# Eight stages and two mixtures of experts: routing rows split by token, the first expert's weights split in the stage in front, routing batches spread

## What is computed

```python
# layer 2: top 2 of 8
probs = softmax(x @ router_w.T); weights, indices = top_k(probs, 2)
weights = weights / (weights.sum() + 1e-6)
h = silu(x @ w13[e][:, :256]) * (x @ w13[e][:, 256:]);  y_e = h @ w2[e]
# layer 3: nucleus, cumulative probability below 0.8, the first always
probs = softmax(x @ Wr + br);  gate = probs * keep
h = relu(x @ W1[e] + b1[e]);   y_e = h @ W2[e] + b2[e]
# both
out = sum over e of gate[:, e] * y_e
```

## Time and profile before

| | us |
|---|---|
| median of 3 runs | 2840.24 (2839.24 to 2847.72) |
| the profiled execution | 2835.16, span 2833.3 |
| stage 6, first to last matmul of the experts | 1428.74 to about 1761 |
| stage 8, the same | 2383.60 to about 2813 |

### The profile page before, as it was taken

One profiled execution on the slowest core, in us unless ns is written; L12 is line 12 of the kernel. 1 busy time (PEld: TensorE's weight loads), 2 busy tenths in 40 slices (PEclk: granted clock), 3 DMA queues, 4 the chain that ended last, 5 costly groups with the idle time before them and its releaser, 6 DMA issues. The chain is left out here.

```text
span 2833.3 us, 35006 instructions
## 1 busy us (share of the span) xinstructions
PE 2458.7 (87%) x12090; PEld 1772.0 (63%) x12090; DVE 1925.9 (68%) x3555; ACT 1459.8 (52%) x3077; POOL 976.1 (34%) x763
## 2 busy tenths in 40 slices
PE   5677778698999999999989998688888886999998
PEld 2554656586888888888867776233333323677776
DVE  6737556776666666666576665499888997766765
ACT  4221222497444444444345555455555553788777
POOL 1000000010222222222025555488888884222221
PEclk8668789899999999999979999799999987999999
DMA  4000000000000000000100000222222230000001
GB/s 172 0 1 0 1 1 1 1 1 15 1 1 1 1 1 1 1 1 1 60 1 1 1 8 0 60 72 84 78 80 82 80 83 15 1 1 1 1 1 30
DMA packets 31169, 66.85 MB, mean 24 GB/s; under 512 B 3200, under 2 KB 7312, under 8 KB 30480
## 3 DMA queue, kind: packets, MB, share of 16 engines
q1 hardware_dynamic: 30960, 64.59, 7.3%
q0 software_dynamic: 32, 0.02, 0.0%
HBM read 61.98 MB, written 2.62 MB: 23 GB/s over the span
## 5 line engine op out<-in xcount | busy, mean ns | idle before, releaser
L192 PE MATMUL ps<-TMPr 128*128 128x512 f32 (+6 forms) x3936 | 1043.1, 413 | 87.0 <-DVE TMPr L208 57.4
L192 PEld LDWEIGHTS ps<-TMPr 128*128 128x128 f32 (+4 forms) x3936 | 736.1, 194 | 402.9 <-issue 176.0
L212 POOL TENSOR_TENSOR TMP<-TMP 128x512 f32<-128x512 f32 (+2 forms) x480 | 619.0, 1314 | 704.3 <-ACT TMP L203 466.3
L192 PE MATMUL ps<-TMP 128*128 128x65 f32 (+4 forms) x4320 | 527.3, 290 | 1.2 <-DVE TMP L207 0.5
L192 PEld LDWEIGHTS ps<-TMP 128*128 128x128 f32 (+3 forms) x4320 | 480.3, 192 | 60.8 <-issue 19.0
L192 PE MATMUL ps<-TMP,W 128*128 128x512 f32 (+5 forms) x720 | 380.6, 655 | 138.6 <-POOL TMP L212 43.3
L203 ACT ACTIVATE TMP<-ps,W 128x256 f32<-128x256 f32 (+2 forms) x512 | 274.4, 580 | 354.7 <-DVE TMP L208 192.7
L208 DVE TENSOR_TENSOR TMP<-ps,TMP 128x512 f32<-128x512 f32 (+1 forms) x434 | 251.4, 603 | 128.0 <-ACT TMP L203 67.8
L192 PEld LDWEIGHTS ps<-TMP,W 128*128 128x128 f32 (+3 forms) x720 | 130.6, 199 | 312.2 <-issue 158.5
L203 ACT ACTIVATE TMPr<-ps,W 128x512 fp32r<-128x512 f32 x352 | 242.4, 689 | 114.4 <-PE ps L192 94.1
L212 POOL TENSOR_TENSOR XT<-XT,XK 128x512 f32<-128x512 f32 x128 | 175.1, 1368 | 324.0 <-DVE XK L211 308.0
(11 more groups left out here) (180 smaller groups left out, 2778.9 us busy)
## 6 DMA issues: line engine op xcount, KB each, us to landing
TMP<-rows SPq DMA_DIRECT2D x168, 256.0 KB, 3.6
W<-wp SPq DMA_DIRECT2D x1, 4124.0 KB, 13.4
W<-wp SPq DMA_DIRECT2D x1, 3072.0 KB, 25.2
W<-wp SPq DMA_DIRECT2D x1, 2136.5 KB, 18.6
XT<-xT SPq DMA_DIRECT2D x4, 512.0 KB, 6.1
out<-XK SPq DMA_DIRECT2D x8, 256.0 KB, 2.3
W<-wp SPq DMA_DIRECT2D x1, 1993.0 KB, 14.2
W<-wp SPq DMA_DIRECT2D x1, 903.0 KB, 9.8
```

The source lines that it names most:

```text
L192: return nc.tensor.matmul(out, lhsT, rhs, start=start, stop=stop, **k)
L212: gtt = lambda o, a, b, op: nc.gpsimd.tensor_tensor(o, a, b, op)
```

## The change

1. **Rows split by token.** Each batch's gate weights are split while tokens are on partitions: DVE casts 128x64 to `WKR` (columns 0 to 7 of each tile's 40) and subtracts for columns 32 to 39. PE turns 40 columns at once, ACT copies all 40 rows to `WT`, and the DVE step of `row` is gone. `gate` waits for the ACT copy (`mw_act`). POOL clears two 128x320 buffers in place of the 40x4096 one.
2. **First expert's weights.** Their high parts are cast on ACT and their low parts subtracted on POOL in the stage in front: at the start of layer norm 5 for stage 6, behind the first norm of stage 7 for stage 8.
3. **Batches and front spread.** The second half of `front` (sum, reciprocal, probabilities) becomes a step at u = 1. Batch 0 stands at u = (2, 2, 2) or (2, 3, 4); batches 1 to 3 at chunks 2, 4, 6. Expert 1's weights come after chunk 5.

```diff
+        def pool(e):
+            if k == 5:
+                first_weights_low(e, 6)
...
-        part = {6: (0, 1, 1), 8: (0, 1, 2)}[k]
+        part, start = {6: (0, 1, 1), 8: (0, 1, 2)}[k], {6: (2, 2, 2), 8: (2, 3, 4)}[k]
...
-                        b = 0 if i == 0 else (i + 1) // 2 if i % 2 else None
-                        if b is not None and b < 4:
-                            plan += [("route", (k, b, r)) for r in range(3) if part[r] == c]
-                        j = i * nd + c - (nd + 1)
+                        u = i * nd + c
+                        if u == 1:
+                            plan.append(("probs", k))
+                        plan += [("route", (k, 0, r)) for r in range(3) if start[r] == u]
+                        if i and i % 2 == 0:
+                            plan += [("route", (k, i // 2, r)) for r in range(3) if part[r] == c]
+                        j = u - (nd + 1)
...
-                if i == 1 and e + 1 < 8:
+                if i == (1 if e else 5) and e + 1 < 8:
                     plan.append(("weights", (k, e + 1)))
...
+    def first_weights_high(e, k):
+        n, u, d = first_w[k]
+        kh = first_wb[k][0]
+        e.wait_ge(s_w[MOE[k]["g"]], 16)
+        acopy(kh[:, 0:512], u)
+        acopy(kh[:, 512:], d).then_inc(*mf_high(k))
+
+    def first_weights_low(e, k):
+        n, u, d = first_w[k]
+        kh, kl = first_wb[k]
+        e.wait_ge(*mf_high.at(k))
+        gtt(kl[:, 0:512], u, kh[:, 0:512].bitcast(F32), ALU.subtract)
+        gtt(kl[:, 512:], d, kh[:, 512:].bitcast(F32), ALU.subtract).then_inc(*mf_low(k))
...
+                high, low = g3(WKR[b % 2], 8)[:, :, 0:8], g3(WKR[b % 2], 8)[:, :, 32:40]
+                e.wait_ge(*at_("scaled" if k == 6 else "kept"))
+                e.wait_ge(*mr_zero.at(k))
+                if b >= 2:
+                    e.wait_ge(*mw_pe.at((k, 2 * b - 3)))
+                copy(high, wk).then_inc(*sig("high"))
+                e.wait_ge(*at_("high"))
+                tt(low, wk, g3(WKF[b % 2], 8)[:, :, 0:8], ALU.subtract).then_inc(*sig("low"))
...
-                        c = 4 * i + j
-                        r = turn(tile(PS[0][0:8, :], j), WK[:, c * 8:c * 8 + 8], w("ident"))
+                        c = 4 * (i % 2) + j
+                        r = turn(tile(PS[0][0:40, :], j), WKF[i // 2 % 2][:, c * 40:c * 40 + 40], w("ident"))
...
-                    e.wait_ge(*mw_dve.at((k, i)))
+                    e.wait_ge(*mw_act.at((k, i)))
...
-                    acopy(ch(WT, a[1])[0:8, :], PS[0][0:8, :]).then_inc(*mw_act(a))
+                    acopy(ch(WT, a[1])[0:40, :], PS[0][0:40, :]).then_inc(*mw_act(a))
...
-            weights(e, 0)
...
-                elif step == "row":
-                    x = ch(WT, a[1])
-                    e.wait_ge(*mw_act.at(a))
-                    minus(x[32:40, :], PS[0][0:8, :], x[0:8, :]).then_inc(*mw_dve(a))
+                elif step == "probs":
+                    probs(e)
...
-            if k == 6:
-                e.wait_ge(*me_w.at((k, 0, "low")))
-                nc.gpsimd.memset(WT.bitcast(F32), 0.0).then_inc(*mr_zero(k))
+            for x in WKF:
+                last = nc.gpsimd.memset(x, 0.0)
+            last.then_inc(*mr_zero(k))
```

More of the change, by code:

```diff
@@ L1738, in build @@
     FRONT = "logits max shifted sum reciprocal probs".split()
-    BATCH = {6: ("top pair pair_reciprocal first", "replaced", "taken kept scaled"),
-             8: ("top cum below always kept_probs", "fill kept_or_fill replaced", "taken kept")}
+    BATCH = {6: ("top pair pair_reciprocal first", "replaced", "taken kept scaled high low"),
+             8: ("top cum below always kept_probs", "fill kept_or_fill replaced", "taken kept high low")}
     LG = mem["TMP"][:, TN - 256:TN]
+    first_w = {6: (768, w("w13")[:, 0:512], w("w2e")[:, 0:256]), 8: (1024, w("W1")[:, 0:512], w("W2")[:, 0:512])}
+    first_wb = {k: [mem["TMPr"][:, TN - 256 - j * n:TN - 256 - (j - 1) * n] for j in (2, 1)] for k, (n, u, d) in first_w.items()}
     def moe_plan(k):
@@ L1792, in build @@
         if st == "front":
-            mr_keys += [(a, "fill")] + [(a, n) for n in FRONT]
+            mr_keys += [(a, n) for n in ["fill"] + FRONT[:3]]
+        elif st == "probs":
+            mr_keys += [(a, n) for n in FRONT[3:]]
         elif st == "route":
@@ L1798, in build @@
     mr_zero = Sig(sem("moe_rows_zeroed"), moe_on)
-    me_w = Sig(sem("moe_weights"), [(k, e, s) for k in moe_on for e in range(8) for s in ("high", "low")])
+    me_w = Sig(sem("moe_weights"), [(k, e, s) for k in moe_on for e in range(1, 8) for s in ("high", "low")])
+    mf_high, mf_low = (Sig(sem("moe_first_weights_" + n), moe_on) for n in ("high", "low"))
     me_sel = Sig(sem("moe_select"), moe_on)
@@ L1817, in build @@
     rows = of(moe_all, "row")
-    mw_pe, mw_act, mw_dve = (Sig(sem("moe_row_" + n), rows) for n in ("pe", "high", "low"))
+    mw_pe, mw_act = (Sig(sem("moe_row_" + n), rows) for n in ("pe", "act"))
     m8_xh, m8_xl = Sig(sem("moe_x_high"), range(NCH)), Sig(sem("moe_x_low"), range(NCH))
     sem.keep()
+    def first_weights_high(e, k):
[10 more added lines that the diff above has]
+        gtt(kl[:, 512:], d, kh[:, 512:].bitcast(F32), ALU.subtract).then_inc(*mf_low(k))
     def moe_stage(k):
@@ L1825, in moe_stage @@
         nw = nu + nd
-        ar, ax = Arena(mem["TMP"], mem["TMPr"], TN - 256), arena_xk()
-        WT, WK = ar(T, 40, FR), ar(256)
-        assert ar.o == XP
+        ar, ax = Arena(mem["TMP"], mem["TMPr"], TN - 256 - 2 * first_w[k][0]), arena_xk()
+        WT, WK = ar(T, 40, FR), ar(64)
+        ar.o = XP
         ar.o += 2 * T
-        wb = [(ar(nw * 128, dt=FR), ar(nw * 128, dt=FR)) for _ in range(2)]
+        wb = [first_wb[k], (ar(nw * 128, dt=FR), ar(nw * 128, dt=FR))]
         s8 = ar(8, 40, FR)
@@ L1839, in moe_stage @@
         pr, V8, R, rp, cum, msk = rt(NT * 16), rt(64), rt(128), rt(64), rt(64), rt(64)
+        WKR = [rt(320, dt=FR) for _ in range(2)]
+        WKF = [x.bitcast(F32) for x in WKR]
         m, s, s2 = SM[:, 96:128], SM[:, 128:160], SM[:, 160:192]
-        l3, p3, w3 = g3(LG, NT), g3(pr, NT)[:, :, 0:8], g3(WK, NT)
+        l3, p3, wk = g3(LG, NT), g3(pr, NT)[:, :, 0:8], g3(WK, 8)
         v3, r3, c3 = g3(V8, 8), g3(R, 8)[:, :, 0:8], g3(cum, 8)
@@ L1947, in bank0_free @@
             if before is not None:
-                e.wait_ge(*(mg_act if before[0] == "gate" else mw_dve).at(before[1]))
+                e.wait_ge(*(mg_act if before[0] == "gate" else mw_act).at(before[1]))
         def pe(e):
@@ L2158, in scan_stage @@
         turning[6], turning[7] = (7, 2), (5, 3)
-        plan = norm(6, 0)
+        plan = norm(6, 0) + [("weights", 8)]
         for j, y in enumerate(prepare(0)):
@@ L2364, in scalar @@
                     acopy(LG[:, 32 * i:32 * i + 32], pn[:, 0:32]).then_inc(*n_lgs(a))
+                elif step == "weights":
+                    first_weights_high(e, 8)
                 elif step == "rows2":
@@ L2500, in pool @@
                     gtt(r, r, power if n == 6 else power[:, 0:4], ALU.pow).then_inc(*n_rt(a))
+                elif step == "weights":
+                    first_weights_low(e, 8)
                 elif step == "dx":
```

16 lines of the change are left out of this document (9 added, 7 removed).

## The result

| | before | after |
|---|---|---|
| median | 2842.22 us (2839.24 to 2847.72, 6 runs) | 2827.68 us (2820.62 to 2831.26, 6 runs) |
| ratio | | 0.9943, 95% interval 0.9926 to 0.996 |
| profiled execution, span | 2835.16, 2833.3 us | 2828.08, 2826.3 us |
| stretch A: norm's last matmul to the end of expert 0, stage 6 | 64.6 us | 57.0 us |
| stretch B: first matmul of stage 8's logits to the end of expert 0 | 79.5 us | 68.6 us |

What follows compares the result with a forecast made beforehand. PE was taken as the bound, by idle time and its lower clock in expert 0 of stages 6 and 8. Gains of 14.2 and 10.2 us, less 1, gave 2835.2 - 23.4 = 2811.8 profiled, 2817 as median; range 2810 to 2831.

Steps and rivals of the forecast that it cites:

- The port: DVE beside POOL: about one 128x64 operation a batch takes 1.27 us in place of 0.23, counted in 3.7 and 3.9.
- The gate's wait is the cost: Expert 0: PE waits before gate matmuls for DVE's 8x512 subtraction, 1.43 to 3.16 us in stage 6; these waits go.
- the wait only moves: Rival, chance 0.07: transposes in expert 0 wait where the gates did; only the earlier starts remain, 2835, no change.
- Stage 6: The stretch of expert 0 in stage 6 ends at 1477.2, 14.2 us earlier.
- Weights in front: PE starts stage 6 1.8 us and stage 8 2.1 us earlier; the work moved into the stages in front costs 0.
- Stage 8: The stretch of expert 0 in stage 8 ends at 2446.4, 10.2 us earlier.
- Batch 0: Stage 6: first transposes 0.8 us later, gate 0 0.6 us earlier; stage 8: gate 0 3.7 us earlier.
- What is late next: DVE in expert 0: PE stalls of 0.3 us in stage 6 and 3.8 us in stage 8.
- I am wrong if PE waits for DVE in each chunk: Sign against the forecast: PE waiting for DVE in each chunk of expert 0; no size given.
- The other signs of being wrong: Waits before the transposes of rows 2, 4 and 6, or scan or norm grown by more than 1 us.
- DVE becomes the bound: Rival, chance 0.18: two more blocked operations a batch need 12.5 us of DVE against slack of about 3; 2826.
- Slower, the clock stays down: Rival, chance 0.04: short waits across expert 0 keep PE at 1.2 GHz; stages 6 and 9 us later, 2855.

Runs made afterwards that it cites:

- the changed kernel again: The changed kernel unaltered, profiled and measured a second time; 2828.87 us, ratio 0.995 to the kernel before.
- early_batch0: Changed kernel with only the probabilities and batch 0 back at the places of the kernel before; 2818.78 us, ratio 0.992.
- short_pool: Changed kernel with POOL's addition of expert 0 to `XT` cut from 512 to 8 columns; 2819.12 us (one run).
- mixed: Changed kernel, probabilities and batch 0 at old places, expert 1's weights behind chunk 6, stage 6 one portion per unit, stage 8 old portions; 2808.5 us, ratio 0.9883.

## Why the prediction was right, and where not

The range held the result and the direction was right; the likeliest value was 11 us too low (a gain of 23.2 forecast, 14.5 measured). The forecast for A and B together was 24.4 us. Against the profile that it was worked out from they gave 18.5, so 5.9 us is the fault of its sum, all of it in stage 6. The rest is below what the profile moves by itself: in a second one of the kernel before A and B were 4.9 us shorter. That the range reached far enough is in part luck, since its slow end was priced by a mechanism that did not act as described (see *The port*).

- *The gate's wait is the cost.* Right, and shown: no 40x512 row has an idle time, and one DVE copy put back into the row costs 22.7 us. The rival "the wait only moves" is out as the whole account; but some of the wait did move, see *Stage 6*.
- *Weights in front.* PE starts stage 6 1.7 us earlier (1.8 forecast) and stage 8 2.2 us earlier (6.55 to 4.31 us behind the logits; 2.1 forecast). The casts on ACT are hidden: two of 0.92 us together at 1402.83, in the idle time before the norm's first work, and the norm is no longer than in the kernel before (24.3 and 21.7 us in either). In the scan stage the rows show them hidden, and the stage's length can't confirm it, as said above.
- *Stage 8* as a whole: the forecast B is 79.5 - 10.2 = 69.3 us, and 68.6 and 69.5 were measured. Its first transposes at 17.3 us are the forecast to 0.1 (2394.3 less 2377.05). The stalls were 2.8 us in place of 3.8, 2.1 of them at the place named, behind chunk 5.
- *Stage 6* is the step that failed: the forecast A is 64.6 - 14.2 = 50.4 us, 57.0 was measured. Of the 6.6 us, 0.9 are the term "Batch 0": the first transposes came at +14.0 us, not +13.1. The product that makes the probabilities took 1.15 us in place of 0.43, beside POOL's low part of 1435.38, and the two products and the low part stood in front as said. The time from there to row 1 was right (7.5 us against 7.3, the lower clock in it). The rest, 5.5 us, is "What is late next": stalls of 0.3 us were forecast and 3.8 came, in six waits, and each cost some 0.2 us more than its idle time (a group begins 0.36 us behind the start of the transposes when nothing waits, and 1.19 us behind it with the wait of 0.60: 0.83 for 0.60), together 5.1 us, so 4.8 more than forecast and nearly the whole of the 5.5. The sum had compared DVE's work with PE's over two chunks, 9.1 of 10.3 us, and so asked only whether DVE keeps up on average. PE waits in each chunk for one certain DVE operation, the product that frees the only output bank, and a batch's portion ahead of it makes that late although DVE has slack. This is what "I am wrong if PE waits for DVE in each chunk" names; it happened in four chunks of stage 6.
- *The other signs of being wrong.* Waits before the transposes of rows 2, 4 and 6 came in a small form: 0.33 and 0.35 us before rows 4 and 6 of stage 6, 0.32, 0.32 and 1.61 before rows 2, 4 and 6 of stage 8. Norm and scan of after were 2.6 and 11.2 us longer, which the kernel before does too in its second profile (2.6 and 7.7), so this sign says nothing.
- *The spread was taken as neutral or good.* It's the largest thing missed. No term of the sum asked what it would be to leave the batches where they were. The later batch 0 alone costs 3.7 and 6.2 us in A and B against the changed kernel again (3.5 and 5.3 against its first profile), the wait before the first transposes being 5.57 and 6.25 us in after against 2.81 and 1.83 in `early_batch0`.
- *The port.* The second case ("DVE becomes the bound", 2826) is close to the measured time, but not by its mechanism. It wanted two more blocked 128x64 operations a batch; in stage 6 there was one in each later batch, three in all (1.21 to 1.31 us) against two before, in stage 8 two (1.11 and 1.08 us, at 2409.49 and 2423.24) against four of 0.95 to 1.30 us, and the new subtraction took 0.22 or 0.23 us in all eight batches. The rule of the Trainium skill (SBUF — State Buffer, Who interferes with whom), that a DVE instruction with two SBUF inputs is blocked while a GpSimd instruction that reads SBUF holds the shared ports, agrees with single rows: the low part of 1455.50 lies over POOL's addition of 1455.06 to 1456.35 and is done at 1456.90, 0.55 us behind it, with 0.68 us of work of its own. The two long ones of stage 8 are TENSOR_SCALAR operations with one input, a kind that the prediction left out (it took all but the cast to have two), and take 0.18 us in the other two batches; that at 2409.49 ends at 2410.60, as POOL's low part does (2409.26 to 2410.55). What the additions cost here is the 4.3 and 1.1 us of DVE that `short_pool` gave back; what POOL's low parts cost was not run.
- *Slower, the clock stays down.* Idles of 0.33 to 1.36 us, in four chunks of stage 6, left the granted clock at 1.00 from 1449 to the end of the stretch, and idles of 0.32 to 1.61 us left it there in stage 8 from 2407 to 2450; so the loss that the Trainium skill describes (TensorE: Matmul & The Clock Gate, A second HAM failure mode: psum-queue depth-cycling) isn't in these stretches. The clock was at 0.50 behind the waits before the first transposes and, as both stages began, from 1423.8 to 1432 and from 2381 to 2388. One reading in the prediction was too coarse: the clock of the kernel before "fell behind waits of 2.8 us and more", but it also fell from 1.00 to 0.50 behind the 2.57 us before 1439.15, and behind the 1.43 us soon after it was at 0.70 and then 0.51 (1444.60 to 1449.00). A wait of 1.36 us that stands by itself in after left it at 1.00.

```profile
1427.40:1430.00 2.60, 2.57 (x6) 2.12 (x7) 1.75 (x6) 0.71 (x1) 0.57 (x2) 0.50 0.00 0
1454.00:1464.00 10.00, 9.40 (x42) 6.65 (x41) 9.16 (x36) 6.21 (x12) 4.65 (x4) 1.00 0.00 0
1464.00:1484.00 20.00, 16.76 (x72) 11.16 (x71) 18.41 (x54) 10.17 (x18) 7.80 (x7) 1.00 0.01 2
2407.00:2450.00 43.00, 40.20 (x175) 29.03 (x174) 38.79 (x142) 34.84 (x58) 13.40 (x11) 1.00 0.00 1
```

## What to carry to other kernels

Ask of a DVE step not how long it takes but what stands in front of it in its queue and who waits behind it: 0.68 us of work, put back eight times a stage, cost 22.7 us, because three times a stage it stood behind a batch. Slack on average hides nothing if PE needs one certain operation in each chunk; look for the buffer with a single copy (here the output bank) and keep bursts away from the operation that frees it. And when a change has several parts, price each against its being left out: without the third part (`old_batches`) A and B were 25.0 us shorter than in the first profile of the kernel before and some 20 shorter than in the second, and the third part gave 7.6 us of it back by A and B, 14 by the medians.

## Of the hardware

A long first wait is paid for again in the matmuls behind it, a short one isn't. Behind 6.25 us of idle in stage 8 of after the granted clock was 0.51 from 2398.4 to 2402.0, and the 25 matmuls from 2399.15 took 7.71 us; in `mixed`, behind 1.91 us, the same 25 took 6.43:

```profile
2398.40:2402.00 3.60, 3.55 (x11) 2.80 (x12) 0.66 (x1) 1.10 (x2) 1.27 (x1) 0.51 0.00 0
...
2389.61 6.43 PE L192 MATMUL ps<-TMPr 128*128 128x512 f32 x25
```

Behind the 2.82 us in stage 6 of `mixed`, 19 matmuls took 6.57 us in place of some 5.05, and behind the 5.57 us of after 7.01. But among the long waits the price doesn't grow with the length: behind 5.70 us in the second profile of the changed kernel the same 25 matmuls took 8.61 us.

And stages whose code was the same moved from execution to execution: in the ten profiles with the first expert's weights made in front the scan took 616.2 to 626.2 us, in the two profiles of the kernel before 613.8 and 621.5, and layer norm 5 took between 21.7 and 24.3 us in both. Two profiles can so differ by some 12 us (10.0 and 2.6) for no reason of their kernels, nearly as much as this change is worth; stretches between fixed places, and medians of many runs, can't be replaced by two spans.
